# Second attention of a four-layer decoder: scores as one fp32 product per head instead of three fp32r products, and a new order around the last key head

## What is computed

```python
hidden = jnp.concatenate([context, latents], axis=1)
q = (latents @ Wq.T).reshape(b, q_len, H, HD)      # H = 16 heads of HD = 96
k = (hidden @ Wk.T).reshape(b, s_len, KV, HD)      # KV = 4 key heads
v = (hidden @ Wv.T).reshape(b, s_len, KV, HD)
...
scores = jnp.einsum('bkgqd,bksd->bkgqs', q, k) * scale
attn = jax.nn.softmax(scores.astype(jnp.float32), axis=-1).astype(q.dtype)
out = jnp.einsum('bkgqs,bksd->bkgqd', attn, v)
return out @ Wo.T
```

## Time and profile before

| | before |
|---|---|
| median of three runs | 1596.52 us |
| profiled execution, its own time | 1596.67 us |
| its span, first to last instruction | 1595.0 us |
| busy: PE, DVE, ACT, POOL | 98%, 61%, 50%, 31% |
| second attention, first score to last projection product of pair 0 | 916 to 981 us |

### The profile page before, as it was taken

One profiled execution on the slowest core, in us unless ns is written; L12 is line 12 of the kernel. 1 busy time (PEld: TensorE's weight loads), 2 busy tenths in 40 slices (PEclk: granted clock), 3 DMA queues, 4 the chain that ended last, 5 costly groups with the idle time before them and its releaser, 6 DMA issues.

```text
span 1595.0 us, 26462 instructions
## 1 busy us (share of the span) xinstructions
PE 1556.8 (98%) x9066; PEld 1280.8 (80%) x9066; DVE 980.7 (61%) x2589; ACT 794.7 (50%) x2279; POOL 492.4 (31%) x358
## 2 busy tenths in 40 slices
PE   9999999999999999999999999999999999999987
PEld 7788888888888888888886788888897788666556
DVE  6762663635636446266477676767676767756677
ACT  5442443434424344244342476667667332288874
POOL 3131320322203213132112713232323533377651
PEclk9999999999999999999999999999999999999999
DMA  5110111101111111011234011020202613000001
GB/s 182 54 44 30 57 43 53 43 30 56 43 39 43 43 56 41 33 51 40 71 93 159 14 40 53 20 72 0 79 1 80 226 54 108 14 15 14 1 2 53
DMA packets 36598, 85.67 MB, mean 54 GB/s; under 512 B 5809, under 2 KB 18737, under 8 KB 34481
## 3 DMA queue, kind: packets, MB, share of 16 engines
q1 hardware_dynamic: 36528, 84.80, 15.9%
HBM read 82.69 MB, written 2.10 MB: 53 GB/s over the span
## 4 chain that ended last, share of the span: by engine, by line
PE 66%; issue 14%; DVE 9%; POOL 5%; ACT 3%; DVEq 2%; DMA 1%; POOLq 0%; SPq 0%; ACTq 0%
PE banks L1284 10%; PE banks L1229 10%; PE banks L1202 10%; PE banks L1210 10%; PE banks L1444 4%; PE banks L1341 3%; PE banks L1324 3%; POOL wo L647 2%; PE banks L1331 2%; PE banks L1664 2%; PE banks L1687 2%; PE banks L1671 1%; ACT p L1079 1%; PE banks L1694 1%; PE banks L1470 1%
## 5 line engine op out<-in xcount | busy, mean ns | idle before, releaser
L559 POOL TENSOR_TENSOR w_q<-w_raw_q,w_q 128x1792 fp32r<-128x1792 f32 x15 | 61.1, 4071 | 479.5 <-ACT w_q L794 479.5
L1284 PE MATMUL banks<-w_o,atT 128*128 128x512 f32 x720 | 180.9, 396 | 0.0
L1202 PE MATMUL banks<-cT,w_k 128*128 128x512 f32 x720 | 178.0, 396 | 0.0
L1229 PE MATMUL banks<-w_v,cT 128*128 128x512 f32 x768 | 177.4, 391 | 0.0
L1229 PEld LDWEIGHTS banks<-w_v,cT 128*128 128x128 f32 x768 | 144.6, 189 | 30.1
L1210 PE MATMUL banks<-xT,w_q 128*128 128x512 f32 x672 | 163.8, 394 | 0.7 <-ACT kT L784 0.7
L2000 DVE TENSOR_TENSOR sA<-banks,pbias 128x512 f32<-128x512 f32 x62 | 42.8, 690 | 186.5 <-PE banks L1324 185.7
L1202 PEld LDWEIGHTS banks<-cT,w_k 128*128 128x128 f32 x720 | 131.9, 188 | 25.5
L1284 PEld LDWEIGHTS banks<-w_o,atT 128*128 128x128 f32 x720 | 131.7, 188 | 25.5
L1210 PEld LDWEIGHTS banks<-xT,w_q 128*128 128x128 f32 x672 | 123.8, 188 | 25.9 <-ACT kT L784 1.1
L853 ACT ACTIVATE sA<-sA,nmA 128x128 f32<-128x128 f32 x248 | 96.4, 392 | 55.7 <-DVE nmA L2005 55.4
(11 more groups left out here) (297 smaller groups left out, 3407.9 us busy)
## 6 DMA issues: line engine op xcount, KB each, us to landing
wo_raw<-in_wo SPq DMA_DIRECT2D x16, 768.0 KB, 4.4
w_raw_v<-in_w0v SPq DMA_DIRECT2D x8, 1024.0 KB, 4.7
w_raw_q<-in_w0q SPq DMA_DIRECT2D x16, 512.0 KB, 3.2
w_raw_k<-in_w0k SPq DMA_DIRECT2D x15, 512.0 KB, 3.4
w_raw_o<-in_w0o SPq DMA_DIRECT2D x15, 512.0 KB, 3.3
cTp<-in_ctxT SPq DMA_DIRECT2D x12, 512.0 KB, 4.6
wq_raw<-in_wq SPq DMA_DIRECT2D x1, 3072.0 KB, 10.3
x_res<-in_x SPq DMA_DIRECT2D x4, 512.0 KB, 11.3
```

Source lines behind the costliest of these rows:

```text
L559: pool.tensor_tensor(w_part[slot][1][:], w_raw[slot][:], w_part[slot][0][:].bitcast(F32), ALU.subtract).then_inc(S(f"w{slot}_lo"), 1)
L1202: mm = pe.matmul(dst, wk_[l][:, c, h * P:(h + 1) * P], cT[r][:, c, half * HT:(half + 1) * HT], start=c == 0 and n == 0, stop=c == DC - 1 a ...
L1229: mm = pe.matmul(dst, cT[l][:, c, b * P:(b + 1) * P], wv_[r][:, c, :], start=n == 0, stop=n == 3 * DC - 1)
L1284: mm = pe.matmul(dst, at_at(l, p, b // 4 * 2 + h)[:, t], w[r][:, h, :], start=start and n == 0, stop=stop and n == 5)
```

## The change

- `scores`: one product per head of `q1` and `k1`, which are now plain fp32 tiles (`F32` for `F32R`), instead of three passes. It waits for `q1_ready` (ACT's copy) instead of `q1_lo`.
- All operations that write `q1_lo` and `k1_lo` are gone from DVE; the value products wait for `k1_ready` instead of `k1_lo`. The memory of the tiles is kept as unused filler, so that all others stay where they were.
- Last key head on PE: the first chunk of `project(2, 1)` follows `project(2, 0)` ahead of the first transposes, and the second and third take the places of the first and second; none is left behind the last attend.
- ACT: `out_high(3)` is cut: its first chunk is done at the end of key head 2, the other two in the old place; `attended(3, 0)` is done whole ahead of `probsT(3, 1)`.
- The low part of the attended rows of key head 3 moves from POOL to DVE (`last_attended`): for batch 0 behind the low parts of the probabilities, for batch 1 behind `next_apply`.
- POOL: the first chunk of `out_rest(3)` waits for the second of ACT's casts, and its waits on `x1_ah` become one form for all key heads.

The diff without the tile declarations:

```diff
@@ POOL, out_rest, split_attended, x1_pool
                 for c in range(NCH):
-                    pool.wait_ge(S("w1_hi"), KV1 + NCH * (KV1 * i + kv) + c + 1)
+
+                    pool.wait_ge(S("w1_hi"), KV1 + NCH * (KV1 * i + kv) + (max(c, 1) if kv == KV1 - 1 else c) + 1)
...
-                pool.wait_ge(S("x1_ah"), 4 * (KV1 * i + kv) + (4 if b == 1 else 2 if kv + 1 == KV1 else 3))
+                pool.wait_ge(S("x1_ah"), 4 * (KV1 * i + kv) + 3 + b)
...
-                    for b in range(2):
-                        split_attended(i, kv, b)
+                    if kv + 1 < KV1:
+                        for b in range(2):
+                            split_attended(i, kv, b)
@@ ACT, x1_act
                     if more:
                         queries(kv + 1, 0, 2)
                     else:
-                        out_high(3)
-                    attended(kv, 0, rest=False)
+                        out_high(3, 1, NCH)
+                    attended(kv, 0, rest=not more)
                     probsT(kv, 1)
                     if more:
                         queries(kv + 1, 2, NCH)
-                    attended(kv, 0, heads=False)
-                    if not more:
+                        attended(kv, 0, heads=False)
+                    else:
                         act.drain()
                         attended_high(kv, 0)
...
                     attended_high(kv, 1)
+                    if kv == 2:
+                        out_high(3, 0, 1)
@@ PE, x1_pe
-                            pe.wait_ge(S("k1_lo"), NCH * i + 2 * b + s + 1)
+                            pe.wait_ge(S("k1_ready"), NCH * i + 2 * b + s + 1)
...
-                            pe.wait_ge(S("q1_lo"), 8 * i + 2 * kv + h // 2 + 1)
+                            pe.wait_ge(S("q1_ready"), 8 * i + 2 * kv + h // 2 + 1)
...
-                        for n, (l, r) in enumerate(PASSES):
-                            mm = pe.matmul(bank(2 + 2 * b + h // 2)[:, (h % 2) * PT2:(h % 2 + 1) * PT2],
-                                           q[l][:, h, b * P:(b + 1) * P], k[r][:, b, :], start=n == 0,
-                                           stop=n == len(PASSES) - 1)
+                        mm = pe.matmul(bank(2 + 2 * b + h // 2)[:, (h % 2) * PT2:(h % 2 + 1) * PT2],
+                                       q1[:, kv % 2, h, b * P:(b + 1) * P], k1[:, kv, b, :], start=True, stop=True)
...
                     if kv == 3:
                         project(2, 0)
+                        project(2, 1, 0, 1)
...
-                            project(2, 1, b, b + 1)
+                            project(2, 1, b + 1, b + 2)
                         attend(kv, b)
-                project(2, 1, 2, NCH)
                 project(3, 0)
@@ DVE, x1_dve (queries_lo, its calls, and the loop over k1_lo are removed)
+                def last_attended(b):
+
+                    k, t = slice(NCH, 2 * NCH), slice(b * P, (b + 1) * P)
+                    dve.wait_ge(S("x1_ah"), 4 * (KV1 * i + KV1 - 1) + 2 * b + 2)
+                    dve.tensor_tensor(at1[1][:, k, t], at1_raw[:, k, t], at1[0][:, k, t].bitcast(F32),
+                                      ALU.subtract).then_inc(S("x1_at"), 1)
+
+                last_attended(0)
                 dve.wait_ge(S("x1_pv"), 8 * i + 8)
                 next_apply(L1X, i)
+                last_attended(1)
```

More of the change, by code:

```diff
@@ L221, in build @@
         ctx_g.close()
-        q1_lo = sb(ctx_f, "q1_part1", [HD1, 2, G1, PT2], F32R)
-        k1_lo = {kv: sb(ctx_f, f"k1_part1_{kv}", [HD1, 2, 2 * P], F32R) for kv in (0, 1)}
-        sb(ctx_f, "f1_rest", [P, 32])
+        sb(ctx_f, "f1_rest", [P, 2 * G1 * PT2 + 2 * 2 * 2 * P + 32])
         ctx_f.close()
@@ L236, in build @@
         ctx_g.close()
-        k1_lo[2] = sb(ctx_b, "k1_part1_2", [HD1, 2, 2 * P], F32R)
+        sb(ctx_b, "tb_f0_rest", [P, 2 * 2 * P])
         tb.update({k: sb(ctx_b, "tb_" + k, [P, D]) for k in ("f1", "f2", "x3")})
@@ L265, in build @@
         ctx_g.close()
-        k1_lo[3] = sb(ctx_b, "k1_part1_3", [HD1, 2, 2 * P], F32R)
+        sb(ctx_b, "hs_rest", [P, 2 * 2 * P])
         nm = sb(ctx_b, "nm", [P, 3, 8])
@@ L289, in build @@
             wo1.append([high_1, sb(ctx_1, f"wo1_1_{k}", [P, NCH, D], F32R)])
-        q1 = sb(ctx_1, "q1", [HD1, 2, G1, PT2], F32R)
+        q1 = sb(ctx_1, "q1", [HD1, 2, G1, PT2])
         at1_hi = sb(ctx_1, "at1_0", [P, 2 * NCH, PT2], F32R)
@@ L296, in build @@
         p1 = sb(ctx_1, "p1", [P, 2, G1, 2 * P])
-        k1 = sb(ctx_1, "k1", [HD1, KV1, 2, 2 * P], F32R)
+        k1 = sb(ctx_1, "k1", [HD1, KV1, 2, 2 * P])
         v1 = sb(ctx_1, "v1", [P, 2, 2, KV1 * HD1], F32R)
@@ L1514, in scores @@
                 def scores(kv, b):
-                    q, k = (q1[:, kv % 2], q1_lo[:, kv % 2]), (k1[:, kv], k1_lo[kv])
                     for h in range(G1):
                         if h % 2 == 0 and b == 0:
-                            pe.wait_ge(S("q1_lo"), 8 * i + 2 * kv + h // 2 + 1)
+                            pe.wait_ge(S("q1_ready"), 8 * i + 2 * kv + h // 2 + 1)
                         if h == 0 and kv > 0:
                             pe.wait_ge(S("x1_ah"), 4 * (KV1 * i + kv - 1) + b + 1)
-                        for n, (l, r) in enumerate(PASSES):
-                            mm = pe.matmul(bank(2 + 2 * b + h // 2)[:, (h % 2) * PT2:(h % 2 + 1) * PT2],
-                                           q[l][:, h, b * P:(b + 1) * P], k[r][:, b, :], start=n == 0,
-                                           stop=n == len(PASSES) - 1)
+                        mm = pe.matmul(bank(2 + 2 * b + h // 2)[:, (h % 2) * PT2:(h % 2 + 1) * PT2],
+                                       q1[:, kv % 2, h, b * P:(b + 1) * P], k1[:, kv, b, :], start=True, stop=True)
                     mm.then_inc(S("x1_s"), 1)
@@ L1552, in project @@
                     if kv == 2 and c0 == 0:
-                        pe.wait_ge(S("q1_lo"), 8 * i + 8)
+                        pe.wait_ge(S("q1_ready"), 8 * i + 8)
                     k = kv % 2
@@ L2180, in x1_dve @@
             def x1_dve(i, last):
[L2181 to L2191, removed]
-                next_stats(i)
[L2194 to L2202, removed]
+                next_stats(i)
                 for s in range(2):
@@ L2236, in x1_dve @@
                 for kv in range(KV1):
-                    more = kv + 1 < KV1
                     row_max(kv, 0)
@@ L2249, in x1_dve @@
                     probs_lo(kv, 0)
-                    if more:
-                        queries_lo(kv + 1, 0, 2)
                     probs_lo(kv, 1)
-                    if more:
-                        queries_lo(kv + 1, 2, NCH)
+                def last_attended(b):
[4 more added lines that the diff above has]
+                last_attended(0)
                 dve.wait_ge(S("x1_pv"), 8 * i + 8)
                 next_apply(L1X, i)
+                last_attended(1)
                 for j in range(2):
```

## The result

The changed kernel takes 1603.54 us (median of five runs, 1602.59 to 1605.19) against 1595.9 for the kernel before in the same rounds: ratio 1.0047, 95% interval 1.0036 to 1.0059. It is slower by 7.6 us; 1603.4 was forecast. The profiled execution took 1602.59 us around a span of 1600.8; it is the fastest of the five.

What follows compares the result with a forecast made beforehand. PE, busy 98% of the span, was taken to bound the kernel. Scores +9.1, first attends -1.0 and last key head -1.2 made +6.9 us on the median 1596.52: 1603.4 us, range 1600 to 1608.

Steps and rivals of the forecast that it cites:

- The score term: Second attention's scores on PE: an fp32 product costs 0.431 us against 0.360 for three passes, 128 heads, +9.1 us.
- The range's 2.2 for switches: Upper bound for switching product kinds on PE: up to 0.11 us in each of 20 score blocks; taken as 0.
- DVE's low parts: Dropping over 10 us a pair of query and key low parts from DVE: almost nothing, since L999 releases the next scores.
- The first attends: First attend of key heads 0 and 1, eight places: DVE gains cover under longer scores, 0.12 us each, -1.0 us.
- The last key head: New order from last head's scores to last projection: waits covered or shortened, -1.2 us over four pairs, between 0 and 6.8.
- The new wait before the attend: Last key head, before the second attend: PE waits 0.6 us for L977, as ACT first copies all first attended rows.
- That waits were the price: Rival: not slower, as the last head's waits (6.8 us) and the attends (1.9) go: +0.4, about 1597; chance 0.11.
- Four passes: Rival: an fp32 product costs four fp32r passes in the scores, +15.4 - 2.2, 1609.7 us; chance 0.05.
- The collision of DVE and POOL: Rival: in the last head DVE's new subtraction is blocked by POOL's L647, +0.7 to +1.3 a pair, 1606 to 1609; chance 0.10.

Runs made afterwards that it cites:

- e3: Changed kernel, but VectorE still computes the low parts of queries and keys, PE still waits for them and nothing reads them: 1605.62 us, ratio 1.0064.
- e6: Changed kernel with ACT's three L999 of batch 0 ahead of the last copy of queries at key heads 0 to 2: 1597.49 us, ratio 1.0014.
- e1: Changed kernel with the old order of the last key head put back, so the score part alone: 1604.76 us, ratio 1.0058.
- e2: Kernel before with only the new order of the last key head, three-pass scores and all low parts kept: 1595.74 us, ratio 0.9998.
- e4: Kernel before with a fourth fp32r pass, low by low, in every head's scores: 1610.40 us, ratio 1.0094.
- e5: Changed kernel with ACT's cast of the next layer's base weights cut in pieces, two before the next rows are stored: 1602.78 us, ratio 1.0043.
- e8: Kernel before (three passes, all low parts) plus the last head's new order, the cut base-weights cast and L999 early at key head 2: 1592.35 us, ratio 0.9979.
- e7: Changed kernel with ACT's copies of the last key head's first attended rows back around the second pair of L977: 1603.40 us, ratio 1.0049.

## Why the prediction was right, point by point

- **The score term** was +9.1, from 0.071 us a head. The four heads of the first block of key head 2, which no wait touches, take 5.93 instead of 5.64 with the filler behind them: 0.29 / 4 = 0.072. Transitions between the two kinds cost nothing: in the second block of key head 2 eight gaps of 0.2155 and six of 0.232 make 3.12, and 3.11 are measured. The first start behind fp32 records alone would mislead: it comes 0.03 behind the last of them, and the one after it 0.43 later. The range's 2.2 for switches was not needed.
- **DVE's low parts** were costed at nothing beyond the attends; e3 gives 0.4 us, and it lies in the last key head. That L999 is late next at the end of key heads 0 to 2 was right, and e6 shows it.
- **The first attends** were to give 1.0; this term was mis-sized. Six products take from 921.79 to 923.43, 1.64 us, where the earlier trace rows have 1.63. The whole gain at key heads 0 and 1 is 0.05 a time, about 0.4 us in all. I had argued that DVE's way to the attend grows by less than PE's, so that some cover is won. The row below shows that none is: DVE begins L2206 at 921.77 and PE the attend at 921.79, and before the change the same two starts are 923.57 and 923.59. From the first score both ways have grown by the same 0.49.

```profile
921.77 1.29 DVE L2206 TENSOR_TENSOR pT_part<-banks,pT 128x512 fp32r<-128x512 f32 x2
```

- **The last key head** was to save 1.2; it saves 2.2 (0.57 less 0.03, four times). e1 and e2 divide it: 0.17 a pair comes with the fp32 scores in the old order (18.74 to 19.14, less 0.57), 0.35 with the new order. The 0.17 is not the covered wait for L653, as I had it in the expectation of e1, since the wait behind it grew by as much. It is DVE's: 0.13 of it is that the transposes come at 6.57 and not at 6.70, and e3, which keeps the low parts, is back at 6.70. Position by position from the first score: transposes 6.57 (I had 6.70), second attend 11.81 (11.93), last projection 13.68 (13.88). The new wait before the attend was sized right; the normalisation reached its end 0.13 sooner than a plain shift of the second row maximum gives (the same 0.13), and everything behind it came with it. DVE's L2232 takes 0.55, as taken from L2208, and the xn step fell to 1.00, as read from the earlier trace rows:

```profile
972.94 1.29 DVE L2206 TENSOR_TENSOR pT_part<-banks,pT 128x512 fp32r<-128x512 f32 x2 [2.54 <-ACT pT L977]
974.14 0.55 DVE L2232 TENSOR_TENSOR at<-at_raw,at 128x384 fp32r<-128x384 f32 x1
974.98 1.00 DVE L1987 TENSOR_SCALAR xn<-x_res,mv,rstd 128x512 f32 x2 [0.29 <-PE banks L1543]
```

- **What the sum did not have** is the layer behind: +1.44. I followed the stage to its last projection and not the queue of ACT and POOL into the next layer, where a late cast of ACT costs 0.6 and a blocked step of DVE 0.8. So the stage's own 6.7 is very near to the 6.9 forecast, by two errors of opposite sign of 0.6 and 1.0 us. The total of 1603.4 also had luck: stage and layer make +8.1 by the distances and the medians +7.6, and the 6.9 was put on a median of 1596.52, where the kernel before took 1595.9 beside the changed one.
- **The rivals.** That waits were the price fell with e2 and the table. Four passes fell with e4. The collision of DVE and POOL did not happen where I had put it (POOL's L646 end at 973.87, DVE's subtraction starts at 974.14), but the mechanism was right and struck in the feed-forward layer behind the stage, on another pair of operations. The Trainium skill ("SBUF — State Buffer", section "Who interferes with whom") has a tensor_scalar among the operations that can take the port shared with GpSimd and be blocked for the whole of a GpSimd instruction. The trace agrees: L1980 ends at 1247.50 and POOL's first addition at 1247.47, L1977 (e1) at 1249.45 and the second at 1249.42, L2151 (e5) at 1249.88 and the second at 1249.85. In e1 the step outlasts two such instructions, the rest of one and the whole of the next.

## What to carry to other kernels

An fp32 product costs 0.43 us for 256 columns here, three fp32r passes 0.36; where PE is busy 98% of the time, taking 54 us from another engine buys next to nothing by itself (0.4 us, e3) against 8 us more on PE. When work is taken from an engine, ask what is late next and move that too: the fp32 form lost 5 to 6 us because ACT's three small copies stood behind one that waited (e6), and the three-pass form lost 2 in the same way (e8). And when a stage is made to end with another queue, follow each engine's queue into the next stage: a cast may now stand ahead of a copy that PE needs, and a tiny step of DVE may fall beside a long one of POOL.

## What the runs showed that I had not expected

- A VectorE operation on 128x2 elements, 0.16 to 0.17 us alone, took 0.53 (before), 0.82 (e4), 1.36 (changed kernel), 1.35 (e5), 2.47 (e1) and 2.65 us (e2, e7) where it met GpSimd additions of 128x512 (1.3 us each), and ended within 0.04 us of the end of one of them; at 2.47 it lasted until the second of two such additions had ended (1249.45 against 1249.42).
- A wait of 2.1 us on PE in a stage that is otherwise full was followed by 5 us at a mean granted clock of 0.66 (e2, one execution). The loss of that feed-forward pair was 4.3 where the changed kernel has 1.4; of the 2.9 between them 1.1 is the longer wait (2.1 against 1.0), the rest goes with the lower clock; in the changed kernel, e1, e3, e6 and e7, with waits of 1.5 us and less in the same place, the clock stayed at the 2.4 GHz level.
